# Scan of a two-layer network: decays from differences of running sums, and the gate product on VectorE

## What is computed

```python
z, xBC, dt_raw = split(layernorm(u) @ in_proj.T)
xBC = silu(conv4(xBC) + conv_b);  x, B, C = split(xBC)
dt = softplus(dt_raw + dt_bias);  dA = dt * A
cum = cumsum(dA)                                # within a chunk
seg = cum[i] - cum[j];  decay = exp(seg) for i >= j, else 0
att = (C[i] . B[j]) * decay * dt[j]
y = att @ x + (C * exp(cum)) @ carried_state + D * x
g = y * silu(z);  g = g * rsqrt(mean(g * g) + eps) * rms_w
out = g @ out_proj.T
```

## Time and profile before

| | |
|---|---|
| median of 3 runs | 5026.35 us (5023.26 to 5029.09) |
| profiled execution | 5039.53 us, its span 5038.0 us |
| TensorE busy over the span | 4661.5 us, 93% |
| VectorE | 4141.8 us, 82% |
| ScalarE | 3503.2 us, 70% |
| GpSimd | 1374.1 us, 27% |
| mean granted TensorE clock | 0.947 |

### The profile page before, as it was taken

One profiled execution on the slowest core, in us unless ns is written; L12 is line 12 of the kernel. 1 busy time (PEld: TensorE's weight loads), 2 busy tenths in 40 slices (PEclk: granted clock), 3 DMA queues, 4 the chain that ended last, 5 costly groups with the idle time before them and its releaser, 6 DMA issues. The chain is left out here.

```text
span 5038.0 us, 108786 instructions
## 1 busy us (share of the span) xinstructions
PE 4661.5 (93%) x35325; PEld 2561.6 (51%) x35325; DVE 4141.8 (82%) x6451; ACT 3503.2 (70%) x6777; POOL 1374.1 (27%) x1290
## 2 busy tenths in 40 slices
PE   8689999999999999999999879999699999965998
PEld 6533333333333333333333357777466666655887
DVE  6689999999999999999999856666577877775554
ACT  3358888888888888888888723333477877744554
POOL 1321111111111111111111133333234344445776
PEclk9879999999999999999999989999799999956999
DMA  8941222222222122212222123232100000044552
GB/s 264 297 113 39 44 52 44 45 43 46 55 44 44 35 53 53 44 39 44 52 44 48 31 87 106 88 116 89 39 29 20 29 20 22 27 160 151 167 165 95
DMA packets 247818, 375.78 MB, mean 75 GB/s; under 512 B 61567, under 2 KB 172690, under 8 KB 238732
## 3 DMA queue, kind: packets, MB, share of 16 engines
q1 hardware_dynamic: 231440, 312.27, 24.7%
q0 software_dynamic: 15904, 57.38, 3.1%
HBM read 241.16 MB, written 136.46 MB: 75 GB/s over the span
## 5 line engine op out<-in xcount | busy, mean ns | idle before, releaser
L833 DVE TENSOR_REDUCE at_mxp<-at_ps_m 128x2 f32<-128x1024 f32 x2092 | 2526.2, 1222 | 78.5 <-PE at_ps_m L886 52.5
L764 ACT ACTIVATE at_prob<-at_ps_s 128x512 f32<-128x512 f32 x4100 | 2227.4, 596 | 331.7 <-PE at_ps_s L876 300.5
L896 PE MATMUL at_ps_o<-at_prob,at_vs 128*32 128x256 f32 x16384 | 1313.9, 393 | 14.0 <-ACT at_osum L770 14.0
L876 PE MATMUL at_ps_s<-at_qs,at_ks 51*128 51x512 f32 x4100 | 1038.0, 501 | 4.7 <-DMA at_qs<-t_largest 4.2
L886 PE MATMUL at_ps_m<-at_ks,at_qs 49*128 49x512 f32 x4184 | 858.4, 406 | 49.7 <-DMA at_ks<-t_alibi 36.5
L876 PEld LDWEIGHTS at_ps_s<-at_qs,at_ks 51*128 51x128 f32 x4100 | 385.1, 184 | 854.2 <-ACT at_prob L764 849.1
L896 PEld LDWEIGHTS at_ps_o<-at_prob,at_vs 128*32 128x32 f32 x16384 | 324.4, 108 | 776.8 <-issue 389.8
L556 POOL TENSOR_TENSOR at_total<-at_total,at_minus 128x16 f32<-128x16 f32 x65 | 190.4, 2929 | 1132.6 <-DMA at_total<-at_osum 1132.6
L886 PEld LDWEIGHTS at_ps_m<-at_ks,at_qs 49*128 49x128 f32 x4184 | 404.6, 190 | 71.6 <-DMA at_ks<-t_alibi 36.9
L1297 ACT ACTIVATE mi_act<-mi_ps_h,mi_b 128x512 f32<-128x512 f32 x131 | 89.9, 686 | 351.4 <-PE mi_ps_h L1385 350.9
L68 DVE TENSOR_TENSOR ex_hidc<-ex_hid,ex_hidc 128x512 fp32r<-128x512 f32 x128 | 154.8, 1219 | 161.6 <-ACT ex_hid L2643 161.6
(11 more groups left out here) (322 smaller groups left out, 6403.6 us busy)
## 6 DMA issues: line engine op xcount, KB each, us to landing
mi_spread<-t_masks SPq DMA_DIRECT2D x68, 512.0 KB, 4.9
t_parts<-pr_parts SPq DMA_DIRECT2D x64, 512.0 KB, 6.8
at_ks<-t_parts SPq DMA_DIRECT2D x102, 256.0 KB
t_buf<-at_blank POOLq DMA_DIRECT2D x64, 384.5 KB, 3.3
at_qs<-t_parts SPq DMA_DIRECT2D x96, 256.0 KB
at_vs<-t_v SPq DMA_DIRECT2D x17, 1024.0 KB
ex_rest<-t_buf SPq DMA_DIRECT2D x16, 1026.0 KB, 5.3
t_v<-pr_vaug SPq DMA_DIRECT2D x64, 256.0 KB, 5.8
```

Source lines behind the costliest of these rows:

```text
L764: nc.scalar.activation(prob[0 if up is None else (t + 1) % 2][:, j, :], ps_s[bank][:, :], ACT.Exp).then_inc(s_read, 1)
L833: nc.vector.tensor_reduce(out[:, s4, k + i, 2 * pair:2 * pair + 2], ps_m[i][:, :, :], AX.X, ALU.max).then_inc(mx_read, 1)
L876: nc.tensor.matmul(ps_s[bank][:, :], ks[s][a:a + QROWS, j // 2, t1 * P:(t1 + 1) * P], qs[s][a:a + QROWS, j // 2, c * T:(c + 1) * T], start ...
L896: last = nc.tensor.matmul(ps_o[32 * j:32 * j + 32, q0:q1], vs[s][:, t, 32 * j:32 * j + 32], prob[t % 2][:, j, q0:q1], start=(t == 0 and ha ...
```

## The change

The decay of a block is now made as a difference of two running sums. One more product of the sums (dA as the weights, `upper` moving) gives the running sums with heads and blocks along partitions and tokens along the row. dA is written twice, with 16 zero columns between, so the result has 48 rows. ScalarE copies it out once in fp32r and once in fp32 and forms `run_m`; GpSimd adds (`running_rows`), so that the first 16 rows hold the sum in fp32r and the last 16 what fp32r left over. GpSimd then spreads the rows by head. For a block TensorE makes two fp32r products of 512 columns, one that adds the sum of the row's token, one that takes away that of the column's. Above the diagonal the exponential may now be large; VectorE limits it to 1 where it multiplies, and the masked scores are zero there. `segment_mask` goes with its 16 activations. The decays of the next chunk's block 0 move from directly behind the sums to behind gates 3, in `A_TURN`, on ScalarE and on TensorE.

The gate product moves from GpSimd to VectorE, directly behind the sum in `own_outputs`, after a drain. SP loads four constant tables at the start of the stage, and GpSimd copies two of them into fp32r.

```diff
@@ -1450,7 +1450,7 @@
...
-          + ["gT1", "cum", "seg0", "z2", "out1", "z3", "gT2", "uT0", "uT1", "gT3", "out2", "out3", "xT0"])
+          + ["gT1", "cum", "z2", "out1", "z3", "seg0", "gT2", "uT0", "uT1", "gT3", "out2", "out3", "xT0"])
@@ -1488,9 +1488,16 @@
...
-        dA = [sb(f"dA{h}", [P, SUB, NH]) for h in range(2)]
+        CR = 3 * SUB * NH
+        dA_rows = [sb(f"dA{h}", [P, 3, SUB, NH]) for h in range(2)]
+        dA = [t[:, 0, :, :] for t in dA_rows]
...
-        segm, decay, att = two("segm", [P, NH, P]), two("decay", [P, NH, P]), two("att", [P, NH, P])
+        decay, att = two("decay", [P, NH, P]), two("att", [P, NH, P])
+        own_rows, minus_rows, head_rows = sb("own_rows", [CR, SUB, P], F32R), sb("minus_rows", [CR, SUB, NH], F32R), sb("head_rows", [CR, NH])
+        run, run_f = [sb(f"run{h}", [CR, P], F32R) for h in range(2)], sb("run_f", [CR, P])
+        run_m = sb("run_m", [CR, P])
+        run_r, minus_low = sb("run_r", [CR, P], F32R), sb("minus_low", [CR, 1])
+        spread_run = [sb(f"spread_run{h}", [CR, NH, P], F32R) for h in range(2)]
@@ -1532,6 +1539,10 @@
...
+                sp.dma_start(decay[0][0:CR, :, :], x["own_rows"].rearrange("r (s c) -> r s c", s=SUB)).then_inc(rows_in, 16)
+                sp.dma_start(decay[1][0:CR, 0, 0:SUB * NH], x["minus_rows"]).then_inc(rows_in, 16)
+                sp.dma_start(head_rows[:, :], x["head_rows"]).then_inc(rows_in, 16)
+                sp.dma_start(minus_low[:, :], x["minus_low"]).then_inc(rows_in, 16)
@@ -1599,7 +1610,16 @@
...
-                    nc.gpsimd.tensor_tensor(dA[h][:, :, :], dts[h][:, :, :], a_neg[:, :].unsqueeze(1).to_broadcast([P, SUB, NH]), ALU.mult).then_inc(dA_done, 1)
+                    for part in (0, 2):
+                        last = nc.gpsimd.tensor_tensor(dA_rows[h][:, part, :, :], dts[h][:, :, :], a_neg[:, :].unsqueeze(1).to_broadcast([P, SUB, NH]), ALU.mult)
+                    last.then_inc(dA_done, 1)
+
+                def running_rows(n, h):
+                    pool.wait_ge(run_out, n + 1)
+                    nc.gpsimd.tensor_tensor(run[h][:, :], run_m[:, :], run_f[:, :], ALU.add)
+                    pool.drain()
+                    nc.gpsimd.tensor_tensor(spread_run[h][:, :, :], run[h][:, :].bitcast(F32).unsqueeze(1).to_broadcast([CR, NH, P]),
+                                            head_rows[:, :].unsqueeze(2).to_broadcast([CR, NH, P]), ALU.mult).then_inc(run_set, 1)
@@ -1607,13 +1627,6 @@
...
-                def gate(i, h, s, old):
-
-                    pool.wait_ge(y_read, i * SUB + s + 1)
-                    if old:
-                        pool.wait_ge(ssq_done, i * SUB + s - 1)
-                    nc.gpsimd.tensor_tensor(g[s % 2][:, :], ysum[s % 2][:, :, :].rearrange("p h c -> p (h c)"), sz[h][:, s, :], ALU.mult).then_inc(g_done, 1)
@@ -1623,25 +1636,29 @@
...
-                        gate(i, h, 0, old)
                         second_root(i + 2)
                         if c == 0:
                             weigh_rows(b, i)
                         softplus_argument(i + 1)
                         softplus_series(i + 1, 1 - h)
-                        gate(i, h, 1, old)
-                        gate(i, h, 2, True)
-                        gate(i, h, 3, True)
+                        running_rows(i + 1, 1 - h)
...
                 nc.gpsimd.memset(twos[:, :, :], 2.0)
+                for h in range(2):
+                    nc.gpsimd.memset(dA_rows[h][:, 1, :, :], 0.0)
...
+                pool.wait_ge(rows_in, 64)
+                nc.gpsimd.tensor_copy(own_rows[:, :, :], decay[0][0:CR, :, :])
+                nc.gpsimd.tensor_copy(minus_rows[:, :, :].rearrange("r s h -> r (s h)"), decay[1][0:CR, 0, 0:SUB * NH])
+                pool.drain()
+                running_rows(0, 0)
@@ -1737,7 +1754,7 @@
...
-                    nc.vector.tensor_tensor(att[r][:, :, :], decay[r][:, :, :], sm[r][:, :].unsqueeze(1).to_broadcast([P, NH, P]), ALU.mult).then_inc(att_done, 1)
+                    nc.vector.scalar_tensor_tensor(att[r][:, :, :], decay[r][:, :, :], 1.0, sm[r][:, :].unsqueeze(1).to_broadcast([P, NH, P]), ALU.min, ALU.mult).then_inc(att_done, 1)
@@ -1750,11 +1767,15 @@
...
                     nc.vector.tensor_tensor(ysum[r][:, :, :], ysum[r][:, :, :], heads(ps_y), ALU.add).then_inc(y_read, 1)
+                    dve.drain()
+                    if old:
+                        dve.wait_ge(ssq_done, i * SUB + s - 1)
+                    nc.vector.scalar_tensor_tensor(g[r][:, :], ysum[r][:, :, :].rearrange("p h c -> p (h c)"), 1.0, sz[h][:, s, :], ALU.mult, ALU.mult).then_inc(g_done, 1)
@@ -1846,18 +1867,13 @@
...
-                def segment_mask(n, h, s, used):
-
-                    act.wait_ge(dA_done, n + 1)
-                    if used is not None:
-                        act.wait_ge(a_done, used + 1)
-                    for k in range(NH):
-                        last = nc.scalar.activation(segm[s % 2][:, k, :], lower[:, :], ACT.Copy, scale=dA[h][:, s, k:k + 1])
-                    last.then_inc(seg_set, 1)
...
                 def sums(turn, h):
                     bank = take(turn, "cum")
+                    nc.scalar.copy(run_r[:, :], bank[0:CR, P:2 * P])
+                    nc.scalar.copy(run_f[:, :], bank[0:CR, P:2 * P])
                     nc.scalar.activation(ex[h][:, :, :, :], bank[:, 0:3 * SUB * NH].rearrange("p (a s h) -> p a s h", a=3, s=SUB), ACT.Exp).then_inc(a_out, 1)
+                    act.drain()
+                    nc.scalar.activation(run_m[:, :], run_r[:, :].bitcast(F32), ACT.Copy, scale=minus_low[:, 0:1]).then_inc(run_out, 1)
@@ -1932,11 +1948,8 @@
...
-                segment_mask(0, 0, 0, None)
-                segment_mask(0, 0, 1, None)
                 sums(None, 0)
                 decays(None, 0, 0, False)
-                segment_mask(0, 0, 2, place(None, "seg0")[0])
@@ -1963,13 +1975,10 @@
...
                         gates(turn, 1 - h, 1)
                         decays(turn, i, 3, True)
-                        segment_mask(i + 1, 1 - h, 0, place(turn, "seg2")[0])
                         projected(turn, h, 0)
                         gated_columns(turn, 1)
                         sums(turn, 1 - h)
                         gate_squares(i, h, 1)
-                        decays(turn, i + 1, 0, True)
-                        segment_mask(i + 1, 1 - h, 1, place(turn, "seg3")[0])
                         gates(turn, 1 - h, 2)
                         conv_silu(i + 1, 1 - h, 4)
                         projected(turn, h, 1)
@@ -1977,6 +1986,7 @@
                         conv_silu(i + 1, 1 - h, 0)
                         conv_silu(i + 1, 1 - h, 1)
                         gates(turn, 1 - h, 3)
+                        decays(turn, i + 1, 0, True)
@@ -2037,16 +2046,15 @@
...
                     for k, m in enumerate((upper, lower, ones)):
-                        last = nc.tensor.matmul(bank[:, k * SUB * NH:(k + 1) * SUB * NH], m[:, :], dA[h][:, :, :].rearrange("p s h -> p (s h)"), start=True, stop=True)
-                    last.then_inc(a_done, 1)
-
-                def decays(turn, i, s):
+                        nc.tensor.matmul(bank[:, k * SUB * NH:(k + 1) * SUB * NH], m[:, :], dA[h].rearrange("p s h -> p (s h)"), start=True, stop=True)
+                    nc.tensor.matmul(bank[0:CR, P:2 * P], dA_rows[h][:, :, :, :].rearrange("p a s h -> p (a s h)"), upper[:, :], start=True, stop=True).then_inc(a_done, 1)
+
+                def decays(turn, i, h, s):
 
                     bank = into(turn, f"seg{s}")
-                    pe.wait_ge(seg_set, i * SUB + s + 1)
-                    for k in range(NH):
-                        last = nc.tensor.matmul(bank[:, k * P:(k + 1) * P], segm[s % 2][:, k, :], upper[:, :], start=True, stop=True)
-                    last.then_inc(a_done, 1)
+                    pe.wait_ge(run_set, i + 1)
+                    nc.tensor.matmul(bank[:, :], own_rows[:, s, :], spread_run[h][:, :, :].rearrange("r h c -> r (h c)"), start=True, stop=False)
+                    nc.tensor.matmul(heads(bank), run[h][:, :], minus_rows[:, s, :].unsqueeze(2).to_broadcast([CR, NH, P]), start=False, stop=True).then_inc(a_done, 1)
@@ -2152,18 +2160,18 @@
...
                         gated_columns(turn, 1)
                         sums(turn, n, g1)
-                        decays(turn, n, 0)
                         gates(turn, g1, 2)
                         project(turn, b, 1)
                         carried(i, h, 3)
                         own(i, c, 3)
                         gates(turn, g1, 3)
+                        decays(turn, n, g1, 0)
                         gated_columns(turn, 2)
...
+    part, sub, head = (k.reshape(-1) for k in np.meshgrid(np.arange(3), np.arange(SUB), np.arange(NH), indexing="ij"))
+    used = part != 1
+    o["own_rows"] = np.repeat(((sub[:, None] == np.arange(SUB)) & used[:, None]).astype(np.float32), P, axis=1)
```

(19 more changed lines are left out.)

6 lines of the change are left out of this document (3 added, 3 removed).

## The result

The changed kernel takes 5049.04 us in the median of 7 runs (5040.19 to 5065.24), against 5029.09 us for the kernel before. The ratio is 1.0039, 95% interval 1.0023 to 1.0055: slower by some 20 us. The forecast was 5025, with a range from 5002 to 5042.

A forecast was written before the change was run, and what follows sets the result against it. TensorE was taken as full, with ScalarE's chain and the VectorE-GpSimd chain to dA almost as long. Its 1.8 us saving is eaten by waits of 1.2 and 0.5, chunk 48.45 against 48.51: 5025 us, range 5002 to 5042.

The forecast's parts named there:

- TensorE's own work: TensorE per chunk: four decay sets save 2.08 us, one more sums product costs 0.25, net 1.83 us saved.
- wait at the last output product: TensorE waits about 1.2 us a chunk for ScalarE's copy of gT3, delayed by the moved decay's table loads.
- wait at the sums: TensorE reaches the sums at +39.8 us, dA comes at +40.3, so it waits 0.5 us a chunk.
- Net on TensorE: 2.08 - 0.25 = 1.83 us: Decay pairs at 0.46 us instead of 0.98 save 0.52 four times; the added sums product costs 0.25.
- The table loads: ScalarE: moving block 0's decay between SiLUs adds two loads of 1.28 us a chunk; TensorE waits about 1.2 us.
- VectorE's 0.9 at own_outputs(0): Gate product and drain on VectorE put about 0.9 us more before whatever stands behind own_outputs.
- The attention product in its new form: VectorE's three-operand attention product takes 0.75 us where it was 0.69, +0.06 four times a chunk.
- GpSimd's series: Softplus steps on GpSimd before dA; 0.2 us taken for meeting one more VectorE instruction, root to dA about 17.2.
- The slower rival: Three to five more GpSimd series steps meet VectorE, dA 1 to 1.5 us later: 5036 to 5049; 0.18 with fp32 case.
- The clock rival: Idle gaps on TensorE bring ten more falls of the granted clock, +14 us, 5039; chance 0.08.
- The signs named: Six table loads, both TensorE waits, none for g, decays 0.46 us, root to dA 17.2, zp median over 536.
- The gate's move: Gate product from GpSimd to VectorE: about 0.9 us more behind own_outputs, and TensorE's waits for g go.

The follow-up runs named there:

- old decays and short series: Kernel before, with the gate product on VectorE and the softplus series without its three highest terms; ratio 0.9944 to the kernel before.
- between and short series: Changed kernel with block 0's decays between the last two output products and the softplus series without its three highest terms; ratio 0.9995.

## Why the prediction was wrong

The waits were forecast rightly, and the term for TensorE's own work was mis-sized. The three terms of the forecast's chunk, and what each measured:

| term | forecast | measured |
|---|---|---|
| TensorE's own work | -1.83 | -0.65 |
| wait at the last output product | +1.2 | +1.05 |
| wait at the sums | +0.5 | +0.42 |
| together | -0.1 | +0.8 |

The wait at the sums is taken from start to start: gT1 ahead of them takes 0.91 us where it takes 0.49 with no wait. Against the start of the decay of block 0, in the chunk shown:

| step | forecast | measured |
|---|---|---|
| last output product starts | +7.0 | 3715.63 - 3708.73 = 6.90 |
| own product 0 | +18.05 | 3726.79: 18.06 |
| root on GpSimd | +23.0 | 3731.64: 22.91 |
| dA | +40.3 | 3749.21: 40.48 |
| sums behind dA | 0 | 0.15 |
| sums to the next decay of block 0 | 8.14 | 3700.14 to 3708.73: 8.59 |
| chunk | 48.45 | 49.22 |

- **The step that failed** is "Net on TensorE: 2.08 - 0.25 = 1.83 us". It measured 0.65 us. Two fp32r products were priced from a row in which six follow each other; alone between fp32 products a visit is 0.56 to 0.64 us and at most places lengthens its neighbours, so the four save 1.17 us and not 2.08. The added sums product was 0.43 for 0.25, with 0.10 more in z2 behind it. In the changed kernel this puts 0.45 us on the path from the sums to the next decay of block 0: 0.25 in the sums, 0.10 in z2 and 0.09 in z3.
- dA was 0.2 late and the sums follow 0.15 behind it. With the 0.45 that is the 0.8 us by which the chunk was longer than forecast. Against the old chunk it is 0.7 us. Taken 15 times that is 11 us of the scan's 16, and the first chunk gave 1. The other 4 lie in chunks with clock falls: over the whole scan the profiles have 85 us of half clock for 79.
- The table loads: forecast 1.2 us, measured 0.9 by the trace and 1.05 by the run without them. VectorE's 0.9 at own_outputs(0): 0.79. Both nearly right, and the loads cannot be seen among the added operations of the diff. The attention product in its new form takes 0.69 us in the median, as the old one did, where 0.75 was taken.
- The rule of the Trainium skill (Vector Engine (DVE) Microarchitecture Reference, points that are easy to get wrong), by which scalar_tensor_tensor with two non-bf16 SBUF sources halves throughput, did not hold here: the gate took 0.69 us, as long as the sum ahead of it, which is a tensor_tensor.
- GpSimd's series: root to dA 17.57 us for 16.88 with one product more; the zp median is 534 ns for 536. The slower rival had the right sign and the right place (TensorE waits for dA in every chunk, so each further bit counts). But behind the second product the series took only 0.3 us more than the forecast had put in, where the rival needed 1 to 1.5, and whether more meetings with VectorE made that is not shown.
- The clock rival: in the two profiles half clock is 54.5 and 56.7 us, so it does not explain the longer chunk. By the clocks of all executions it may be 5 to 11 of the 20 us, beside some 12 from the chunk; that part is not settled, since the two kernels' clocks come from different series. It accounts for why none of the repairs paid off.
- The signs named: six table loads in a chunk, both waits and no wait for g came, and the chunk stayed under 49.5 us. The decay products were 0.56 to 0.64 instead of 0.46, root to dA 17.57 instead of 17.2, and the zp median did not rise. TensorE did wait for the running rows, once, in the prologue: 4.9 us in place of 2.7 for the masks, 2.2 more where 1 was forecast.
- The gate's move: forecast as a cost of 0.9 us on the chain and the end of the waits for g. Alone it changes nothing measurable; in company with the new decays it is a gain of some 19 us, since g no longer stands behind dA.
- By the profiles the scan with old decays and short series is 11 us shorter than with new ones, by the ratios the kernels lie 25 us apart. The clocks of all their executions fit the larger number: 245 us lost for 273. Not settled is what it is in the new decays that lowers the clock, beyond that more columns in the pairs raise it again.

## What to carry to other kernels

Price a matrix product of another form where it will stand, between its neighbours, and not from a row in which its like follow each other: of four places two gave the saving and two did not. Before work on a full engine is shortened, follow the chains that are nearly as long, and ask of an activation that moves which functions it will stand between. The cheaper edit was in the chain that TensorE waited for: six short steps less on an engine that was 27% busy gave 0.66%, at the price of three terms of the series. And look at the granted clock of all executions before a shorter chunk is taken for a faster kernel.

## What the runs showed of the hardware

- A visit of two fp32r products of 512 columns between fp32 products took 0.64 us (0.56 ahead of the scores), a visit of four 1.09; the fp32 products beside it took about 0.1 us longer at most places. At the carried product of block 3 they did not: it and the pair together took 1.50 us, the carried product alone 1.05.
- TensorE at 99.8% busy by the profile (728.89 of 730 us) still had a mean granted clock of 0.96. A full queue did not keep the clock up; the same chunks with fp32 decays had 0.98. Over all executions and the whole span it was 0.946 for 0.951.
- In these two runs, behind the first chunk, every fall inside a chunk began 20.0 to 22.3 us behind the start of the sums; the 16 products of four columns end at 19.7 and 20.1.
- One stretch at 1.2 GHz in a chunk cost about 1.1 to 1.9 us (48.2 to 49.3 between and short series, 49.2 to 51.2 in the changed kernel).
